# A gated attention and FFN block: a new order of the opening, weight loads moved, and unused multiplications on TensorE

## The chip, the cores and the metric

The kernel runs on one core of a Trainium2 chip. The metric is the device time of one execution in microseconds. The kernel is one program in which every engine has its own queue of instructions: TensorE (PE) multiplies, VectorE (DVE), ScalarE (ACT) and GpSimd (POOL) work on vectors, SyncE (SP) issues nearly all transfers. Engines wait for each other by semaphores only.

## The reference

Two sequences of 2048 tokens with 512 features (`x`), and for each a context of 128 rows. Cut to what matters:

```python
q = layernorm(x) @ Wq + bq ;  k = ctx @ Wk + bk ;  v = ctx @ Wv + bv     # 16 heads of 32
x = x + tanh(g_xattn) * (softmax(q k^T / sqrt(32)) v @ Wo + bo)
h = concat([layernorm(x), -layernorm(x)])
h = relu(s0 * h @ sign(k0)) * 2          # sign(k) is +1 where k is true, else -1; 1024 -> 2048
h = relu(s1 * h @ sign(k1)) * 2          # 2048 -> 2048
x = x + tanh(g_ffn) * s2 * h @ sign(k2)  # 2048 -> 512
```

## The kernel before

The tokens go through in 16 chunks of 256 (two tiles of 128 rows, TT = 2). Most values are kept as a high and a low float16 part, so that a product is two or three matmuls; the parts are made by ScalarE (high, by a copy) and VectorE (low, by a subtraction).

**The opening** handles the attention of chunk 0 and prepares what all chunks share. Its order is the list FIRST, written by hand: each engine walks the list and does its part of every item. The items are: LN and N1 (layernorm), T1 (turning the normed rows, by transposes on TensorE), CQ (splitting Wq: ScalarE Wq_hi L507, VectorE Wq_lo L938), CX (turning the context), Q n (queries of head group n, L1111 to L1113), QP n (their split, L537, L541, L793), K n (keys, L1059), KP n (their split: VectorE L915, ScalarE L499, GpSimd L426), KM n (keys masked by head: VectorE L931 for group 0, GpSimd L432 for the others), V (values of a batch, L1066), VP (their split, L921, L503, L923), SCALARS (gates and signs, VectorE L699 to L728), XB (bias of the residual, GpSimd L439), CO and CL (splitting Wo, L510 and L943), W0 (weights of the first FFN layer, L957 to L962), and for each of U = 8 units (four heads of 128 tokens) S (scores, L1094; VectorE takes the maximum, L797), EX (exponentials, ScalarE L520), PT (turning the probabilities: TensorE L1036, ScalarE L564, VectorE L744) and PV (the sum over values: TensorE L1120 and L1121, VectorE L752 to L759). CT, WO, N2 and T2 end the attention of the chunk. For unit k the loop over k puts S k+1, EX k and PV k-2, then what the table BETWEEN holds for k, then PT k-1.

**The loop** runs over FFN chunks f. SLOTS lists 44 steps of the FFN: eight L0 (first layer, L1210 and L1211), two L2P (end of the last chunk), then four groups q of seven L1 steps (second layer) with L2 steps (third layer, L1260 and L1261) of the group before between them. The attention of the next chunk is woven in by slot number (WEAVE, QUERIES): unit u has S at slot 10 + 2u, PS (split of the probabilities, L598 and L801, then a transposing transfer into PT) at 11 + 2u and PV at 15 + 2u. In chunk 0 the second layer is plain (`plain_product`, L1181 and L1183); from chunk 1 on it is done in seven products of block sums (L1243 and L1244), for which VectorE makes four sums of weight blocks for each group. `weight_step(q, step)` does that: step 0 makes signs of the loaded k1 (L973), steps 1 to 4 the sums (L977, L979, L983, L987). LATE_WEIGHTS says at which slot of chunk 0 or 1 each step stands. `load_k1(engine, q)` issues the two transfers of group q (L304).

W1 group 2 first holds Wv and group 3 holds Wq, so those loads come after their last use. In the SyncE queue the load of group 2 stands here, in chunk 0:

```python
                    if f == 0 and slot == ("L1", 1, P2):
                        sp.wait_ge(v_done, BATCHES)
                        load_k1(sp, 2)
```

That is slot 18; VectorE's step (2, 0), which waits for it, is also at slot 18.

## Time and profile before

| | |
|---|---|
| median of 3 runs | 1595.79 us (1595.55 to 1598.28) |
| the profiled execution: its time, its span | 1598.79 us, 1597.0 us |
| TensorE busy | 1533.0 us, 96% of the span |
| VectorE, ScalarE, GpSimd busy | 59%, 42%, 11% |
| mean granted clock of TensorE | 0.987 of full speed |

Times in the trace are microseconds from the start of the span. The granted clock is the share of TensorE's full 2.4 GHz that the chip let through; its lower level is 0.5, 1.2 GHz. The opening lasts until 88.26, when the first L1210 matmul starts; FFN chunk 0 lasts until 204.78.

### The profile page before, as it was taken

The numbers are of one execution on the slowest core, as the hardware profiler recorded it, in microseconds if no ns is written. First come the engines' busy times: TensorE is split into PE (matmuls) and PEld (weight loads), VectorE is DVE, ScalarE is ACT, GpSimd is POOL, SyncE is SP. The second block draws the span as 40 slices with busy tenths as digits, with TensorE's granted clock in tenths as the row PEclk, the third lists the DMA queues.
The fourth block names the chain that finished last, engine by engine and source line by source line (L and its number), as shares of the span: only waits on it lengthen the run. The fifth ranks groups of instructions, "written<-read, shape, count | busy, mean of one in ns | idle before, by whom it ended". The sixth has DMA issues, their size and how long they took to land.

```text
span 1597.0 us, 46107 instructions
## 1 busy us (share of the span) xinstructions
PE 1533.0 (96%) x19856; PEld 1302.6 (82%) x19856; DVE 939.8 (59%) x1938; ACT 674.1 (42%) x1568; POOL 168.0 (11%) x273
## 2 busy tenths in 40 slices
PE   5697989999999999999999999999999999999998
PEld 3476678888988888898888988888898888889887
DVE  4675875655656565565656556565655656565441
ACT  3343154452535445253544435254443525444231
POOL 2200202011020200102020110202011020201100
PEclk9799999999999999999999999999999999999999
DMA  7443225242332425343242423324252432424100
GB/s 224 96 103 73 47 71 90 48 94 61 94 67 63 99 46 99 58 94 68 79 83 51 97 55 97 65 81 81 51 98 55 97 65 75 87 50 98 28 29 14
DMA packets 278226, 120.95 MB, mean 76 GB/s; under 512 B 243464, under 2 KB 259848, under 8 KB 277896
## 3 DMA queue, kind: packets, MB, share of 16 engines
q1 hardware_dynamic: 275960, 117.48, 34.2%
q8 instruction: 156, 2.56, 0.7%
q10 hardware_dynamic: 2064, 0.53, 0.1%
q14 instruction: 46, 0.38, 0.1%
HBM read 37.76 MB, written 16.78 MB: 34 GB/s over the span
## 4 chain that ended last, share of the span: by engine, by line
PE 79%; DVE 9%; ACT 5%; issue 3%; DMA 3%; POOL 1%; SPq 0%; DVEq 0%; ACTq 0%; POOLq 0%
PE bank L1243 19%; PE bank L1244 19%; PE bank L1210 6%; PE bank L1211 6%; PE bank L1260 6%; PE bank L1261 6%; ACT Pf L520 2%; PE bank L1111 2%; PE bank L1112 2%; PE bank L1113 2%; PE bank L1127 2%; PE bank L1129 2%; PE bank L1128 2%; DVE nmax L797 2%; DMA PT<-Phl 1%
## 5 line engine op out<-in xcount | busy, mean ns | idle before, releaser
L1243 PE MATMUL bank<-H,W 128*128 128x128 f16 x6720 | 778.3, 219 | 5.2 <-ACT C L613 4.0
L1244 PE MATMUL bank<-H,W 128*128 128x128 f16 x6720 | 778.0, 219 | 0.0
L1243 PEld LDWEIGHTS bank<-H,W 128*128 128x128 fp8e5 x6720 | 655.4, 98 | 17.4 <-ACT C L613 9.8
L1244 PEld LDWEIGHTS bank<-H,W 128*128 128x128 fp8e5 x6720 | 657.4, 98 | 7.1
L1210 PE MATMUL bank<-hT,W 128*128 128x256 f16 x1024 | 228.5, 274 | 7.3 <-DVE h L852 5.4
L1211 PE MATMUL bank<-hT,W 128*128 128x256 f16 x1024 | 228.5, 274 | 0.0
L520 ACT ACTIVATE Pf<-bank,nmax 128x128 f32<-128x128 f32 x512 | 146.4, 369 | 155.2 <-DVE nmax L797 144.8
L1260 PE MATMUL bank<-W,h 128*128 128x512 fp8e5 x512 | 195.2, 381 | 1.6 <-DVE h L845 1.6
L1261 PE MATMUL bank<-W,h 128*128 128x512 fp8e5 x512 | 195.0, 381 | 0.0
L469 POOL TENSOR_TENSOR attn<-pvs 128x128 f32<-128x128 f32 x120 | 76.0, 633 | 1016.5 <-DVE pvs L810 1016.5
L837 DVE TENSOR_TENSOR C<-bank,C 128x256 f32<-128x256 f32 x180 | 76.3, 424 | 161.7 <-ACT C L613 89.8
L613 ACT ACTIVATE C<-bank 128x256 f32<-128x256 f32 x180 | 69.9, 388 | 212.8 <-PE bank L1244 212.8
L801 DVE SCALAR_TENSOR_TENSOR Phl<-Pf,Phl 128x512 f16<-128x512 f32 x120 | 82.6, 689 | 93.4 <-ACT Phl L598 93.3
L832 DVE TENSOR_TENSOR H<-Fp,H 128x896 f16<-128x896 f32 (+1 forms) x128 | 135.3, 1059 | 0.8 <-ACT H L604 0.8
L1210 PEld LDWEIGHTS bank<-hT,W 128*128 128x128 fp8e5 x1024 | 100.7, 98 | 19.6 <-issue 7.7
L638 ACT ACTIVATE Fp<-bank 128x512 f32<-128x512 f32 x128 | 76.5, 597 | 94.0 <-PE bank L1211 92.7
L609 ACT ACTIVATE H<-Fp 128x896 f16<-128x896 f32 x120 | 113.4, 945 | 1.8 <-DVE Fp L868 1.7
L845 DVE SCALAR_TENSOR_TENSOR h<-C,h 128x256 f16<-128x256 f32 x180 | 76.5, 425 | 60.8 <-ACT h L676 29.1
L1211 PEld LDWEIGHTS bank<-hT,W 128*128 128x128 fp8e5 x1024 | 100.6, 98 | 11.9
L797 DVE TENSOR_REDUCE nmax<-bank 128x4 f32<-128x512 f32 x128 | 87.6, 685 | 23.2 <-PE bank L1155 15.5
L1260 PEld LDWEIGHTS bank<-W,h 128*128 128x128 f16 x512 | 50.3, 98 | 53.6 <-issue 2.8
L1261 PEld LDWEIGHTS bank<-W,h 128*128 128x128 f16 x512 | 50.3, 98 | 51.8 <-issue 0.8
(129 smaller groups left out, 1919.4 us busy)
## 6 DMA issues: line engine op xcount, KB each, us to landing
Qst<-q_bounce SPq DMA_DIRECT2D x120, 128.0 KB, 2.8
Y<-in_x_dram SPq DMA_DIRECT2D x16, 512.0 KB, 3.8
...
```

Of the source, the lines that this page charges most:

```text
L520: last = nc.scalar.activation(Pf[:, n % 2, j * P:(j + 1) * P], bank[:, j * P:(j + 1) * P], ACT.Exp, bias=nmax[:, n % 2, j:j + 1], scale=1.0)
L609: nc.scalar.activation(H0[:, 0, i], Fp[:, i % 3, 1:8, :], ACT.Copy).then_inc(l0_hi, 1)
L638: nc.scalar.activation(Fp[:, n % 3, 0:4, :], banks[n % 3][:, :].rearrange("p (b n) -> p b n", b=4), ACT.Relu)\
L797: V_.tensor_reduce(nmax[:, n % 2, :], bank[:, :].rearrange("p (j k) -> p j k", j=4), AX.X, ALU.max, negate=True).then_inc(s_max, 1)
L801: V_.scalar_tensor_tensor(out=Phl[:, n % 2, 1, :], in0=Pf[:, n % 2, :], scalar=PS, in1=Phl[:, n % 2, 0, :], op0=ALU.mult, op1=ALU.subtract)\
L832: V_.tensor_tensor(H0[:, 1, i, rows, :], Fp[:, i % 3, of, :], H0[:, 0, i, rows, :], ALU.subtract)\
L1210: mm(o, w, hT[:, k, :], start=k == 0, stop=False)
L1211: last = mm(o, w, hT[:, KT + k, :], start=False, stop=k == KT - 1)
L1243: mm(o, w, H0[:, 0, i, b_of, :], start=first, stop=False, skip_group_check=True)
L1244: last = mm(o, w, H0[:, 1, i, b_of, :], start=False, stop=i == PAIRS - 1, skip_group_check=True)
L1260: mm(banks[3 + t][:, :], hi, w2, start=q == 0 and h == 0 and jj == 0, stop=False)
L1261: last = mm(banks[3 + t][:, :], lo, w2, start=False, stop=q == GROUPS - 1 and h == 1 and jj == 1)
```

## The change

It rewrites the order of the opening, moves two loads and several weight steps, and adds multiplications whose result nobody reads.

- The table BETWEEN becomes EARLY (ahead of S and EX of the unit) and MIDDLE. KP and KM stand early, K one or more units ahead of its KP. QD is a new name for VectorE's part of QP, so that it can stand later. SCALARS stands ahead of Q 0; the product of bo with its gate is an item of its own, BO.
- V of a batch is two halves of 256 columns, V 0 and V 1 for batch 0.
- EX n of the opening waits for PT n-2 on TensorE, no longer for its low part on VectorE.
- SyncE issues the k1 load of group 3 right behind group 0's, and that of group 2 at slot 9 instead of 18.
- Three weight steps, (2, 4), (3, 2) and (3, 3), go from chunk 0 to chunk 1; others stand at every second slot.
- WARM n is n matmuls of 512 columns on zeros in PT, into bank 5: 14 ahead of T1, 6 ahead of Q 0, 5 ahead of WO 0, 7 behind T2.

```diff
+    FIRST = first(("LN", 0), ("LN", 1), ("N1", 0), ("N1", 1), ("WARM", 14), ("T1", 0), ("T1", 1), ("CQ", 0), ("CQ", 1), ("CQ", 2),
+                  ("CQ", 3), ("CX", 0), ("CX", 1), ("WARM", 6), ("SCALARS", 0), ("Q", 0), ("Q", 1), ("QP", 0), ("QD", 0),
...
+    EARLY = {1: first(("KP", 2), ("KM", 2)), 2: first(("QP", 2), ("VP", 0)), 3: first(("KP", 3), ("KM", 3)),
...
+    MIDDLE = {0: first(("V", 0), ("K", 2)), 1: first(("V", 1), ("Q", 2)), 2: first(("QD", 2), ("K", 3)),
...
     for k in range(U + 2):
-        FIRST += first(*((kind, k + ahead) for kind, ahead in (("S", 1), ("EX", 0), ("PV", -2)) if 0 <= k + ahead < U))
-        FIRST += BETWEEN.get(k, [])
+        FIRST += EARLY.get(k, [])
+        FIRST += first(*((kind, k + ahead) for kind, ahead in (("S", 1), ("EX", 0)) if 0 <= k + ahead < U))
+        FIRST += first(("PV", k - 2)) if k > 2 else []
+        FIRST += MIDDLE.get(k, [])
         FIRST += first(("PT", k - 1)) if 0 <= k - 1 < U else []
+        FIRST += first(("PV", 0)) if k == 2 else []
         FIRST += first(("CT", k - 8)) if k >= 8 else []
...
-                     26: (1, 2), 28: (3, 0), 29: (1, 3), 31: (1, 4), 32: (2, 1), 34: (2, 2), 35: (2, 3), 36: (2, 4),
-                     37: (3, 1), 39: (3, 2), 41: (3, 3)}, {9: (3, 4)})
+                     26: (1, 2), 28: (3, 0), 30: (1, 3), 32: (1, 4), 34: (2, 1), 36: (2, 2), 38: (2, 3), 40: (3, 1)},
+                    {11: (2, 4), 15: (3, 2), 19: (3, 3), 23: (3, 4)})
...
+            sp.wait_ge(wq_lo, KT)
+            load_k1(sp, 3)
             sp.wait_ge(n1_ready, NT)
...
             load_k1(sp, 1)
-            sp.wait_ge(wq_lo, KT)
-            load_k1(sp, 3)
...
-                    if f == 0 and slot == ("L1", 1, P2):
-                        sp.wait_ge(v_done, BATCHES)
+                    if f == 0 and slot == ("L2P", GROUPS - 1, 1):
+                        sp.wait_ge(v_done, 2 * BATCHES)
                         load_k1(sp, 2)
...
-                if a or n >= 2:
+                if a == 0 and n >= 2:
+                    act.wait_ge(p_turned, n - 1)
+                if a:
                     act.wait_ge(p_lo, nth(a, NU, n - 2))
...
+            V_.memset(PT[:, 1], 0.0).then_inc(zeros_made, 1)
...
+                if kind == "WARM":
+                    pe.wait_ge(zeros_made, 1)
+                    idle = PT[:, 1].rearrange("p a n -> p (a n)")
+                    for _ in range(n):
+                        mm(banks[5][:, :], idle[:, 0:P], idle[:, 0:4 * P], start=True, stop=True)
```

TensorE's queue at its start, from T1 over CX (the rows that read R) to the first query matmul, before:

```order
L1036 MATMUL bank<-ident,xn 128x128 [waits n1_ready]
L1036 MATMUL bank<-ident,xn 128x128 x3
L1036 MATMUL bank<-ident,xn 128x128 [waits n1_ready]
L1036 MATMUL bank<-ident,xn 128x128 x3
L1036 MATMUL bank<-ident,R 128x128 [waits ctx_in,ident_made]
L1036 MATMUL bank<-ident,R 128x128 x7
L1111 MATMUL bank<-xT,Wq_hi 128x256 [waits first_lo,wq_lo,ctx_taken]
```

The same place in the changed kernel (its lines are numbered some 9 to 16 higher; L1055 is WARM):

```order
L1055 MATMUL bank<-PT 128x512 [waits zeros_made]
L1055 MATMUL bank<-PT 128x512 x13
L1045 MATMUL bank<-ident,xn 128x128 [waits n1_ready]
L1045 MATMUL bank<-ident,xn 128x128 x3
L1045 MATMUL bank<-ident,xn 128x128 [waits n1_ready]
L1045 MATMUL bank<-ident,xn 128x128 x3
L1045 MATMUL bank<-ident,R 128x128 [waits ctx_in,ident_made]
L1045 MATMUL bank<-ident,R 128x128 x7
L1055 MATMUL bank<-PT 128x512 [waits zeros_made]
L1055 MATMUL bank<-PT 128x512 x5
```

The multiplications of zeros stand ahead of T1 and behind CX; nothing else moved between them. VectorE's queue between the low parts of PT 0 and PT 1 (L744), before; the rows from L699 to L728 are SCALARS with the product of bo:

```order
L699 TENSOR_SCALAR c<-scal 128x2 [waits scalars_in]
L701 TENSOR_SCALAR c<-c 128x2 [waits const_step]
L704 TENSOR_SCALAR c<-c 128x1 [waits const_tanh,const_step]
L705 TENSOR_SCALAR c<-c 128x1
L706 TENSOR_SCALAR c<-c,scal 128x1
L707 TENSOR_TENSOR c<-scal,c 128x2
L709 TENSOR_SCALAR c<-c 128x1 [waits const_step]
L712 TENSOR_SCALAR bo_b<-bo_b,c 128x512 [waits bo_in]
L719 TENSOR_SCALAR w_mask<-scal 128x1
L723 SCALAR_TENSOR_TENSOR w_mask<-w_mask 128x1 [waits const_step] x2
L728 TENSOR_TENSOR w_mask<-w_mask,eleventh_mask 128x1 [waits masks_made,const_step]
L744 SCALAR_TENSOR_TENSOR PT<-bank,PT 128x512 [waits p_hi,const_step]
```

And between the same two rows (L749) in the changed kernel:

```order
L749 SCALAR_TENSOR_TENSOR PT<-bank,PT 128x512 [waits p_hi]
L926 TENSOR_TENSOR Phl<-bank,Phl 128x512 [waits v_done,bv_in]
L928 SCALAR_TENSOR_TENSOR V<-Phl,V 128x16x32 [waits v_hi]
L802 TENSOR_REDUCE nmax<-bank 128x4 [waits s_done]
L798 TENSOR_TENSOR Qhl<-Qf,Qhl 128x256 [waits q_split]
L749 SCALAR_TENSOR_TENSOR PT<-bank,PT 128x512 [waits p_hi]
```

SCALARS has left this place; the split of V (L926, L928) and the low part of Q 2 (L798) stand in it. SyncE's queue in FFN chunk 0 around the k1 load of group 2 (L304), before:

```order
L367 DMA Qst<-q_bounce 64x1024 [waits s_done,q_kept1]
L367 DMA Qst<-q_bounce 64x1024
L373 DMA_TRANSPOSE PT<-Phl 128x8x128 [waits p_lo,pv_done]
L304 DMA W<-in_L_ffn_k_dram 128x16x64 [waits v_done]
L304 DMA W<-in_L_ffn_k_dram 128x16x64
L373 DMA_TRANSPOSE PT<-Phl 128x8x128 [waits p_lo,pv_done] x4
```

And after (the load is L309, q_bounce and Qst are the queries on their way, PT the probabilities):

```order
L372 DMA Qst<-q_bounce 64x1024 [waits s_done,q_kept1]
L372 DMA Qst<-q_bounce 64x1024
L309 DMA W<-in_L_ffn_k_dram 128x16x64 [waits v_done]
L309 DMA W<-in_L_ffn_k_dram 128x16x64
L363 DMA q_bounce<-Qhl 4x32x256 [waits q_lo]
L363 DMA q_bounce<-Qhl 4x32x256
L378 DMA_TRANSPOSE PT<-Phl 128x8x128 [waits p_lo,pv_done]
```

The load went from behind the fourth PT transfer to ahead of the first, and ahead of the last query's transfer.

## Rows read from the trace of the kernel before

**Rows 1.** The page of the profile: span and busy time of the engines.

```profile
span 1597.0 us, 46107 instructions
...
PE 1533.0 (96%) x19856; PEld 1302.6 (82%) x19856; DVE 939.8 (59%) x1938; ACT 674.1 (42%) x1568; POOL 168.0 (11%) x273
```

**Rows 2.** Busy time by stretch, in us from the start of the span.

```profile
core 0: us, PE busy (x) PEld busy (x) DVE busy (x) ACT busy (x) POOL busy (x), PEclk, DMA share, GB/s
42.30:72.90 30.60, 19.99 (x142) 15.48 (x140) 16.52 (x39) 13.72 (x37) 5.08 (x7) 0.74 0.51 121
132.30:204.80 72.50, 56.36 (x441) 41.12 (x439) 54.67 (x61) 14.09 (x32) 10.86 (x14) 0.91 0.31 63
204.80:297.40 92.60, 92.17 (x1219) 78.39 (x1220) 56.12 (x116) 41.01 (x96) 9.80 (x16) 0.98 0.36 72
```

**Rows 3.** A wait of TensorE before 88.3 us: total, times, longest.

```profile
PE bank L1094 <- POOL h L432: 9.9, 2, 5.0
```

**Rows 4.** Busy time and granted clock of TensorE alone, by stretch.

```profile
core 0: us, PE busy (x), PEclk, DMA share, GB/s
8.55:12.20 3.65, 3.65 (x16) 1.00 0.87 267
15.00:20.00 5.00, 5.00 (x24) 1.00 1.00 384
30.80:32.10 1.30, 1.30 (x13) 1.00 0.45 75
142.40:147.10 4.70, 4.70 (x22) 0.51 0.30 56
204.80:208.60 3.80, 3.80 (x19) 0.52 0.00 0
```

**Rows 5.** Timeline of VectorE, opening: start, length, instruction, idle before, releaser.

```profile
18.61 0.42 DVE L793 TENSOR_TENSOR Qhl<-Qf,Qhl 128x256 f16<-128x256 f32 x1 [3.13 <-ACT Qf L541]
...
34.26 0.69 DVE L744 SCALAR_TENSOR_TENSOR PT<-bank,PT 128x512 f16<-128x512 f32 x1 [0.59 <-ACT PT L564]
...
37.56 0.16 DVE L699 TENSOR_SCALAR c<-scal 128x2 f32<-128x2 f32 x1
...
42.32 0.69 DVE L744 SCALAR_TENSOR_TENSOR PT<-bank,PT 128x512 f16<-128x512 f32 x1
...
63.31 0.69 DVE L744 SCALAR_TENSOR_TENSOR PT<-bank,PT 128x512 f16<-128x512 f32 x1 [0.78 <-ACT PT L564]
...
67.34 0.69 DVE L744 SCALAR_TENSOR_TENSOR PT<-bank,PT 128x512 f16<-128x512 f32 x1 [0.92 <-ACT PT L564]
...
72.16 0.69 DVE L744 SCALAR_TENSOR_TENSOR PT<-bank,PT 128x512 f16<-128x512 f32 x1 [1.52 <-ACT PT L564]
```

**Rows 6.** Timeline of ScalarE, one step of the opening.

```profile
64.10 1.14 ACT L520 ACTIVATE Pf<-bank,nmax 128x128 f32<-128x128 f32 x4 [0.82 <-DVE PT L744]
...
66.07 0.61 ACT L510 ACTIVATE Wo_hi<-H 128x512 f16<-128x512 f32 x1
...
66.71 0.60 ACT L564 ACTIVATE PT<-bank 128x512 f16<-128x512 f32 x1
```

**Rows 7.** Timeline of TensorE: three waits in the first FFN chunk.

```profile
142.40 0.24 PE L1120 MATMUL bank<-V,PT 128*128 128x65 f16 x1 [7.54 <-ACT Pf L520]
...
164.43 0.22 PE L1120 MATMUL bank<-V,PT 128*128 128x65 f16 x1 [2.76 <-DMA PT<-Phl]
...
204.78 0.37 PE L1210 MATMUL bank<-hT,W 128*128 128x256 f16 x1 [5.38 <-DVE h L852]
```

**Rows 8.** Timeline of the SyncE queue: two loads of k1.

```profile
15.77 12.10 SPq L304 DMA_DIRECT2D W<-in_L_ffn_k_dram  x2
...
132.34 2.23 SPq L304 DMA_DIRECT2D W<-in_L_ffn_k_dram  x2
```

**Rows 9.** Timeline of VectorE, first FFN chunk: two weight steps.

```profile
139.28 1.29 DVE L973 TENSOR_SCALAR W<-W,w_mask 128x2048 uint32<-128x2048 uint32 x1 [8.34 <-DMA W<-in_L_ffn_k_dram]
...
201.75 2.28 DVE L983 TENSOR_TENSOR W<-W 128x2048 fp8e5<-128x2048 fp8e5 x1
```

More of the change, by code:

```diff
@@ new lines, in gated_block_kernel @@
+    EARLY = {1: first(("KP", 2), ("KM", 2)), 2: first(("QP", 2), ("VP", 0)), 3: first(("KP", 3), ("KM", 3)),
+             4: first(("QP", 3)), 5: first(("KP", 4)), 6: first(("KP", 5)), 7: first(("KP", 6)), 8: first(("KP", 7))}
+    MIDDLE = {0: first(("V", 0), ("K", 2)), 1: first(("V", 1), ("Q", 2)), 2: first(("QD", 2), ("K", 3)),
+              3: first(("Q", 3), ("BO", 0)), 4: first(("QD", 3), ("XB", 0), ("K", 4), ("CO", 0)),
+              5: first(("XB", 1), ("K", 5), ("CL", 0), ("CO", 1)), 6: first(("K", 6), ("CL", 1), ("CO", 2)),
+              7: first(("K", 7), ("CL", 2), ("CO", 3)), 8: first(("CL", 3)), 9: first(("W0", 0))}
@@ L131, in gated_block_kernel @@
         FIRST += first(("CT", k - 8)) if k >= 8 else []
     FIRST += [(1, ("LN", 0)), (1, ("LN", 1))]
-    FIRST += first(("WO", 0), ("WO", 1), ("N2", 0), ("N2", 1), ("V", 1), ("T2", 0), ("T2", 1))
+    FIRST += first(("WARM", 5), ("WO", 0), ("WO", 1), ("N2", 0), ("N2", 1), ("V", 2), ("V", 3), ("T2", 0), ("T2", 1),
+                   ("WARM", 7))
     FIRST_ITEMS = [item for a, item in FIRST if a == 0]
@@ L729, in follow_sign @@
                     .then_inc(const_step, 1)
-                dve.wait_ge(const_step, 9)
+                dve.wait_ge(const_step, 8)
             def attend_first(item):
@@ L790, in attend @@
                             in1=xs[:, k % 2, 0, :], op0=ALU.mult, op1=ALU.subtract).then_inc(xs_lo, 1)
-                if kind == ("QP" if first else "Q"):
+                if kind == ("QD" if first else "Q"):
                     dve.wait_ge(q_split, nth(a, NG, n))
@@ L1045, in begin @@
                 before = user_before(FIRST_ITEMS, FIRST_BANK, item)
-                if before is not None:
+                if before is not None and not (kind == "V" and n % 2):
                     pe.wait_ge(*released(before, 0))
@@ L1064, in begin @@
                         pe.wait_ge(wv_in, 16)
+                    b, half = divmod(n, 2)
+                    columns = slice(half * D // 2, (half + 1) * D // 2)
                     for k in range(KT):
-                        last = mm(bank[:, :], ctxT[:, k, n * P:(n + 1) * P], Wv_f[:, k, :],
-                                  start=k == 0, stop=k == KT - 1)
+                        last = mm(bank[:, columns], ctxT[:, k, b * P:(b + 1) * P], Wv_f[:, k, columns],
+                                  start=k == 0, stop=k == KT - 1, skip_group_check=True)
                     last.then_inc(v_done, 1)
```

31 lines of the change are left out of this document (12 added, 19 removed).

## The prediction

> **What bounds the kernel now.** I read the page first: TensorE is busy for 1533.0 of the 1597.0 us of the span [rows 1]. The busy times by stretch say where the other time is. From 204.8 us on a chunk takes about 92.6 us, and TensorE is busy for 92.17 of them: nothing that frees another engine can help there. The opening is different: from 42.3 to 72.9 us TensorE is busy for 19.99 of 30.60 us, at a mean granted clock of 0.74. The second part of FFN chunk 0, from 132.3 to 204.8 us, has 56.36 busy of 72.50 us, and VectorE is busy for 54.67 of them [rows 2]. Since everything behind is bound by TensorE, a microsecond taken out of either stretch ends the kernel a microsecond earlier, if no new wait takes its place.
>
> The waits of TensorE and the timelines name the causes. In the opening it waited 9.9 us, in two pieces, for the masked keys of GpSimd [rows 3]. The step from one low part of PT to the next is the beat of the softmax units: PT 0 stands at 34.26, PT 1 at 42.32, PT 7 at 72.16 us [rows 5], so seven steps took 37.9 us. In the first of them VectorE did SCALARS, from 37.56 to the PT row at 42.32, 4.8 us. In chunk 0 there are three waits: 7.54, 2.76 and 5.38 us [rows 7]. The first has its root in VectorE, which sat 8.34 us for a k1 load [rows 9] that SyncE issued only at 132.34 [rows 8]. After two of them the clock is at its lower level for busy stretches of 4.7 and 3.8 us [rows 4].
>
> **The change part by part.** The sums are made against the profiled execution, 1598.79 us, which is 1.8 above its span and 3.0 above the median of the three runs.
>
> *Up to the first scores.* Fourteen zero matmuls fill the start. At the lower clock 24 matmuls of 256 columns took 5.00 us, at the higher 12 took 1.30 us [rows 4], so one of 512 columns is 0.42 or 0.22 us. Fourteen are at most 5.9 us and end before the first transposes, which wait for VectorE's xn until 8.5 us: they cost nothing. If the clock is up when Q 0 and Q 1 come, these 24 matmuls take 2.6 instead of 5.0 us: 2.4 off. CX 0 no longer stands between the four splits of Wq: 0.6 off. SCALARS, 3.7 us without the product of bo, now stands ahead of the split of Q 0, where VectorE sat 3.13 us [rows 5]; its small instructions ran while GpSimd masked keys, so I take half a microsecond of it as uncovered. The six zero matmuls in front of Q 0 are 1.3 to 2.5 us long and have VectorE's Wq splits as cover (TensorE waited 2.8 us there); were that gone they would cost that much. I take 2.5 off, bounds 0 and 4.
>
> *The eight softmax units.* With SCALARS out and keys split one unit ahead, a step should shrink to what VectorE and ScalarE do in series. From the rows: low part of PT 0.6 us, VectorE's part of KP and the hop 0.4, ScalarE's KP 0.2, EX 1.0 (from 64.10 on, without its pipelined end), the Wo split 0.6, the high part of PT 0.6 [rows 5, 6]: 3.4 us. The steady steps of before, such as 63.31 to 67.34, took 4.0, since PV on VectorE stood in the chain in front of KP. Seven steps at 3.5 are 24.5 us. TensorE then works less than half of the last two steps, as it did before, so I expect the lower clock there, with a key block and a PT turn at half speed on the chain: 1.5 us more. 26.0 instead of 37.9 us: 11.9 off, bounds 8 and 14. GpSimd's masks of 2.1 us start right after the keys and end two units before their scores; they are what is late next if the keys are.
>
> *From PT 7 to the first layer.* The path stays. Five zero matmuls stand ahead of WO 0, whose operands are ready: 1.1 to 2.1 us in the way, of which part comes back since WO 0 then runs sooner at full clock. The seven behind T2 are 1.5 to 2.9 us and lie beside the splits of T2, for which TensorE waited 1.9 us; without that cover they cost it all. V as halves has the same columns. I take 0.4 lost, bounds 3 lost and 1.5 won. The opening gives 2.5 + 11.9 - 0.4 = 14.0 us.
>
> *The load of group 2.* It goes to slot 9, nine steps of some 2 us before its use, against 6.3 us that it took to land. The 7.54 us wait goes, and with it 4.7 us at the lower clock, half of which is 2.35: 9.9 off. In SyncE's queue two query pieces and the PT transfers now stand behind it. It held the queue for 2.23 us at its old place and, in a full queue, a like pair for 12.10 [rows 8]. I take 1 us lost, bounds 0 and 8.
>
> *The late wait of 2.76 us* and a short one of 0.46 before it come from VectorE catching up after its 8.34 us; they have 3.2 us at the lower clock behind them, 1.6 lost. Of these 4.8 I take 3.5 as gone.
>
> *Three weight steps less in chunk 0.* Each is 2.28 us [rows 9], and VectorE's last h row before chunk 1 stood behind them. The end wait of 5.38 us falls to the bare split of the last block, which I put at 1.5 us, the length of ScalarE's high part and VectorE's low part: 3.9 off, and 3.8 us at the lower clock become 1.9: 5.8 off. In chunk 1 VectorE has 56.12 busy of 92.6 us [rows 2]; three steps make it 63. They stand on the slots of PS, so each can delay a PT transfer by 2.28 us, with four slots to its PV. I take 1.5 lost, bounds 0 and 6.8 (all three in full).
>
> Chunk 0 and 1 give 9.9 - 1 + 3.5 + 5.8 - 1.5 = 16.7 us. The whole is 14.0 + 16.7 = 30.7 off 1598.79, which is 1568.1; at the median, 1595.8 - 30.7 = 1565.
>
> *A rule against the warming.* From 8.55 to 12.2 us TensorE turned blocks without a gap, and at 15 to 20 us it still ran 24 matmuls in 5.00 us, the pace of the lower clock, though the profile has no reading of the granted clock that early and prints 1.00 [rows 4]. The Trainium skill, "TensorE: Matmul & The Clock Gate", Part 4: PE-mode transpose, says that transposes don't count as TensorE activity in the way of matmuls. By that rule, the trace agrees, the gain of the fourteen would be lost again during T1 and CX.
>
> **The rivals.**
> - *The warming doesn't hold.* The clock falls between the fourteen and Q 0, since transposes and a 2 us gap lie between. For it: 3.7 us of transposes did not raise the clock. Against it: six zero matmuls follow at once. Then the 2.4 us of Q stay, and the five ahead of WO 0 cost their 2 us: 1565 + 2.4 + 2 = 1569. The rule of the Trainium skill quoted above says this.
> - *Chunk 0 stays bound by VectorE.* It is busy for 54.67 of 72.50 us there [rows 2]; less 6.8 it has 47.9, but its steps alternate with waits for ScalarE. If the steps between slots 18 and 28 still make TensorE wait, the 3.5 don't come and chunk 1 costs its 6.8: 1565 + 3.5 + 5.3 = 1574.
> - *Keys on the chain of the units.* If each KP waits for its K on TensorE, a step gets the PV, the key block and a hop, 1.3 us at full clock: seven steps make 9 us, 1574. Against it: K stands a whole step ahead.
> - *Slower.* The early load holds SyncE's queue with queries and PT transfers behind it. At 12.10 us, less some 3.5 of slack, TensorE waits 8.6, which only takes the place of the wait removed: 1574. It ends above before only if the queue stands for more than 35 us, the 30.7 won and the slack; no row shows a pair of loads of 1 MB held so long.
> - *No effect:* the opening's gain is given back by a k1 or x transfer that is as late as before. The loads are issued by semaphores that move with the opening, and TensorE waited for no load of the opening.
>
> **How the numbers follow.** The forecast as summed has a chance of 0.6, the first rival 0.12, the second 0.12, the third 0.08, the slower one 0.03 (of which 0.02 above before), no effect 0.02, a mixture beyond these 0.03. The bounds of the terms that are free (opening 4 either way, chunk 0 and 1 some 5) give 1556 to 1574 for the forecast; up to 1578 takes in most of the rivals. A measurement of this kernel can tell a change of 0.2%, 3.2 us. Faster by more: 0.96; within: 0.02; slower: 0.02.
>
> **What would show it.** L1226, the first layer, starts near 74 us instead of 88.3. SCALARS lies before 20 us, the PT rows follow each other by 3.4 to 4 us. Query matmuls before 20 us run at 0.11 us each, or at 0.21 if the first rival is right. The wait of 7.54 us is gone and VectorE's step (2, 0) has no transfer ahead of it. The second chunk starts near 174 us. From there chunks of 92 to 93 us, the first of them with small waits where the three steps lie. The prediction is wrong if the first layer starts after 79 us, or if waits of several microseconds for PT transfers stand in chunk 0 or 1.

## The result, and the profile after

The changed kernel takes 1571.78 us, the median of four runs (1570.59 to 1572.85), against 1597.00 us of the kernel before beside it (1595.55 to 1598.28): a ratio of 0.9842, interval 0.9825 to 0.9859, 1.6% faster. The profiled execution took 1571.66 us.

The page of the changed kernel, the lines that answer to [rows 1]:

```profile
span 1569.8 us, 46204 instructions
...
PE 1530.4 (97%) x19904; PEld 1302.2 (83%) x19904; DVE 938.9 (60%) x1939; ACT 672.3 (43%) x1568; POOL 168.8 (11%) x273
```

The span is 27.2 us shorter and TensorE's busy time 2.6 us, but the small second number hides a larger one. The kernel without the zero matmuls (the first experiment below) is as fast, and its page has TensorE busy for 1522.1 us, 10.9 less than before, at a mean granted clock of 0.996 instead of 0.987. So some 11 us of the gain are busy time, most of it presumably matmuls that no longer run at the lower clock, and some 16 are idle time that is gone; the zero matmuls fill 8.3 us of what is left idle without them.

The busy times by stretch of the changed kernel, for the stretches that answer to those of [rows 2]: PT 0 to PT 7, the second part of chunk 0, and chunk 1 to the point that lies 92.7 us behind its start.

```profile
core 0: us, PE busy (x) PEld busy (x) DVE busy (x) ACT busy (x) POOL busy (x), PEclk, DMA share, GB/s
30.60:55.70 25.10, 16.38 (x157) 12.26 (x156) 21.66 (x47) 15.60 (x45) 6.72 (x9) 1.00 0.57 135
118.00:177.70 59.70, 53.75 (x435) 39.71 (x433) 46.92 (x55) 13.94 (x32) 12.83 (x14) 0.97 0.26 52
177.70:270.40 92.70, 88.38 (x1188) 75.75 (x1189) 60.99 (x117) 40.15 (x95) 10.44 (x16) 1.00 0.33 73
```

The reader sees three things. PT 0 to PT 7, seven steps, takes 25.10 us at a granted clock of 1.00; the row of before starts at PT 1, and its six steps had 30.60 us at 0.74. The end of chunk 0 is 59.70 us with 5.95 idle, where 72.50 had 16.14 idle. And chunk 1, which had 0.43 us idle in 92.60, now has 4.32 in 92.70: something was pushed there.

The timeline of TensorE in the changed kernel: the first matmul of the first layer in chunks 0, 1 and 2 (L1226), and the two longest waits (in brackets, with what ended them). They answer to [rows 7].

```profile
73.92 0.27 PE L1226 MATMUL bank<-hT,W 128*128 128x256 f16 x1 [0.37 <-DVE hT L743]
...
140.94 0.19 PE L1136 MATMUL bank<-V,PT 128*128 128x65 f16 x1 [2.68 <-DMA PT<-Phl]
...
177.69 0.27 PE L1226 MATMUL bank<-hT,W 128*128 128x256 f16 x1 [1.63 <-DVE h L857]
...
221.58 0.23 PE L1259 MATMUL bank<-H,W 128*128 128x128 f16 x1 [2.34 <-ACT C L620]
...
274.84 0.27 PE L1226 MATMUL bank<-hT,W 128*128 128x256 f16 x1
```

The waits of TensorE before 73.95 us, to be held against [rows 3]: those for GpSimd's masked keys are not among them any more. What is left between the units is TensorE waiting for VectorE's low part of each PT, the beat of the softmax units itself.

```profile
PE bank L1136 <- DVE PT L749: 6.8, 6, 1.6
PE bank L1045 <- DVE attn L764: 1.9, 2, 1.2
```

VectorE's opening, to be held against [rows 5]: SCALARS starts at 15.70 instead of 37.56, PT 0 stands at 30.61, PT 1 at 34.13, PT 7 at 55.71.

```profile
15.70 0.17 DVE L706 TENSOR_SCALAR c<-scal 128x2 f32<-128x2 f32 x1 [0.35 <-DMA scal<-in_L_ffn_s_dram]
...
30.61 0.69 DVE L749 SCALAR_TENSOR_TENSOR PT<-bank,PT 128x512 f16<-128x512 f32 x1 [3.41 <-ACT PT L571]
...
34.13 0.68 DVE L749 SCALAR_TENSOR_TENSOR PT<-bank,PT 128x512 f16<-128x512 f32 x1
...
55.71 0.68 DVE L749 SCALAR_TENSOR_TENSOR PT<-bank,PT 128x512 f16<-128x512 f32 x1
```

Seven steps took 25.1 us instead of 37.9. SyncE's queue, against the second row of [rows 8]: the k1 load of group 2 is issued at 96.12 instead of 132.34 and holds the queue for 2.43 us.

```profile
96.12 2.43 SPq L309 DMA_DIRECT2D W<-in_L_ffn_k_dram  x2
```

Before the experiments, the account by place, from the starts of the first layer in each chunk (before: 88.26, 204.78, 299.50 us; after: the rows above):

| | before | after | difference |
|---|---|---|---|
| opening | 88.26 | 73.92 | -14.34 |
| chunk 0 | 116.52 | 103.77 | -12.75 |
| chunk 1 | 94.72 | 97.15 | +2.43 |
| chunk 2 to the end | 1297.5 | 1295.0 | -2.5 |

The last row has the same code in both kernels. In the profiles of the twelve experiments it lies between 1294.0 and 1296.3 us, so some 2 us of the 27.2 belong to the one execution of before that was profiled. The other three rows give 24.7 us, and the medians 25.2.

### The profile page after: what moved, and what is told of

It is laid out like the page before. It is cut to its first block, busy times and chain, and to the rows that moved or that the text cites. A ratio compares the mean times of both kernels' runs of the same rounds, so it can differ in the third digit from the quotient of the medians.

```text
span 1569.8 us, 46204 instructions
## 1 busy us (share of the span) xinstructions
PE 1530.4 (97%) x19904; PEld 1302.2 (83%) x19904; DVE 938.9 (60%) x1939; ACT 672.3 (43%) x1568; POOL 168.8 (11%) x273
## 4 chain that ended last, share of the span: by engine, by line
PE 87%; DVE 6%; ACT 3%; DMA 2%; issue 1%; SPq 0%; POOL 0%; DVEq 0%; ACTq 0%; POOLq 0%
PE bank L1259 22%; PE bank L1260 22%; PE bank L1226 7%; PE bank L1227 7%; PE bank L1276 7%; PE bank L1277 6%; PE bank L1143 2%; PE bank L1144 2%; PE bank L1145 2%; PE bank L1127 2%; PE bank L1129 2%; PE bank L1128 2%; PE bank L1171 1%; PE bank L1199 1%; PE bank L1197 1%
## 5 line engine op out<-in xcount | busy, mean ns | idle before, releaser
L1226 PE MATMUL bank<-hT,W 128*128 128x256 f16 x1024 | 226.8, 273 | 2.0 <-DVE h L857 1.6
L527 ACT ACTIVATE Pf<-bank,nmax 128x128 f32<-128x128 f32 x512 | 145.9, 368 | 139.2 <-DVE nmax L802 137.5
L806 DVE SCALAR_TENSOR_TENSOR Phl<-Pf,Phl 128x512 f16<-128x512 f32 x120 | 82.5, 688 | 92.0 <-ACT Phl L605 91.9
L1226 PEld LDWEIGHTS bank<-hT,W 128*128 128x128 fp8e5 x1024 | 100.2, 98 | 14.2 <-issue 2.7
L1227 PEld LDWEIGHTS bank<-hT,W 128*128 128x128 fp8e5 x1024 | 100.2, 98 | 11.3
L802 DVE TENSOR_REDUCE nmax<-bank 128x4 f32<-128x512 f32 x128 | 87.5, 683 | 17.5 <-PE bank L1171 16.6
```

The source lines that it names most:

```text
L527: last = nc.scalar.activation(Pf[:, n % 2, j * P:(j + 1) * P], bank[:, j * P:(j + 1) * P], ACT.Exp, bias=nmax[:, n % 2, j:j + 1], scale=1.0)
L802: V_.tensor_reduce(nmax[:, n % 2, :], bank[:, :].rearrange("p (j k) -> p j k", j=4), AX.X, ALU.max, negate=True).then_inc(s_max, 1)
L806: V_.scalar_tensor_tensor(out=Phl[:, n % 2, 1, :], in0=Pf[:, n % 2, :], scalar=PS, in1=Phl[:, n % 2, 0, :], op0=ALU.mult, op1=ALU.subtract)\
L1226: mm(o, w, hT[:, k, :], start=k == 0, stop=False)
L1227: last = mm(o, w, hT[:, KT + k, :], start=False, stop=k == KT - 1)
```

## The experiments

The positions are those of each kernel's profiled execution. Each group was timed beside the kernel before on one chip; the ratio is to that, and kernels of different groups are best compared by it.

| kernel | median us | ratio, interval | first layer at | chunk 1 at | chunk 0 |
|---|---|---|---|---|---|
| changed kernel | 1571.78 | 0.9842, 0.9825 to 0.9859 | 73.92 | 177.69 | 103.77 |
| no zero matmuls | 1572.11 | 0.9844, 0.9831 to 0.9858 | 73.56 | 177.27 | 103.71 |
| only the 14 | 1570.66 | 0.9834, 0.9821 to 0.9848 | 73.12 | 176.93 | 103.81 |
| only the 6 | 1570.67 | 0.9833, 0.9820 to 0.9847 | 74.08 | 177.62 | 103.54 |
| without the 5 and 7 | 1570.58 | 0.9834, 0.9820 to 0.9847 | 75.33 | 179.05 | 103.72 |
| load back at slot 18 | 1580.01 | 0.9895, 0.9880 to 0.9910 | 74.42 | 186.31 | 111.89 |
| old weight slots | 1573.68 | 0.9851, 0.9836 to 0.9865 | 75.77 | 183.21 | 107.44 |
| before, load at slot 9 | 1588.85 | 0.9951, 0.9934 to 0.9968 | 88.74 | 196.52 | 107.78 |
| before, SCALARS early | 1596.10 | 0.9998, 0.9988 to 1.0007 | 87.76 | 204.22 | 116.46 |
| SCALARS back behind PT 0 | 1573.02 | 0.9843, 0.9829 to 0.9858 | 73.17 | 176.96 | 103.79 |
| keys late | 1580.69 | 0.9893, 0.9876 to 0.9909 | 80.84 | 184.41 | 103.57 |
| five steps on odd slots | 1568.26 | 0.9816, 0.9801 to 0.9830 | 74.06 | 174.33 | 100.27 |
| combined | 1566.44 | 0.9803, 0.9788 to 0.9817 | 72.78 | 173.04 | 100.26 |

### Do the zero matmuls give anything?

Four kernels leave out all of them, or keep only some. All:

```diff
-    FIRST = first(("LN", 0), ("LN", 1), ("N1", 0), ("N1", 1), ("WARM", 14), ("T1", 0), ("T1", 1), ("CQ", 0), ("CQ", 1), ("CQ", 2),
-                  ("CQ", 3), ("CX", 0), ("CX", 1), ("WARM", 6), ("SCALARS", 0), ("Q", 0), ("Q", 1), ("QP", 0), ("QD", 0),
+    FIRST = first(("LN", 0), ("LN", 1), ("N1", 0), ("N1", 1), ("T1", 0), ("T1", 1), ("CQ", 0), ("CQ", 1), ("CQ", 2),
+                  ("CQ", 3), ("CX", 0), ("CX", 1), ("SCALARS", 0), ("Q", 0), ("Q", 1), ("QP", 0), ("QD", 0),
...
-    FIRST += first(("WARM", 5), ("WO", 0), ("WO", 1), ("N2", 0), ("N2", 1), ("V", 2), ("V", 3), ("T2", 0), ("T2", 1),
-                   ("WARM", 7))
+    FIRST += first(("WO", 0), ("WO", 1), ("N2", 0), ("N2", 1), ("V", 2), ("V", 3), ("T2", 0), ("T2", 1))
```

> The changed kernel without any of the 32 zero multiplications. Theory (the new order and the moved loads are the gain, the warming is worth little): Q 0 and Q 1 run at 0.21 us a matmul, the first layer starts 0 to 2.5 us later than the 73.9 us of the changed kernel, the kernel takes 1572 to 1574 us. Rival (the warming carries a good part of the 14 us of the opening): first layer after 77 us, 1576 us or more.

The second keeps only the 14 ahead of T1:

```diff
-                  ("CQ", 3), ("CX", 0), ("CX", 1), ("WARM", 6), ("SCALARS", 0), ("Q", 0), ("Q", 1), ("QP", 0), ("QD", 0),
+                  ("CQ", 3), ("CX", 0), ("CX", 1), ("SCALARS", 0), ("Q", 0), ("Q", 1), ("QP", 0), ("QD", 0),
...
-    FIRST += first(("WARM", 5), ("WO", 0), ("WO", 1), ("N2", 0), ("N2", 1), ("V", 2), ("V", 3), ("T2", 0), ("T2", 1),
-                   ("WARM", 7))
+    FIRST += first(("WO", 0), ("WO", 1), ("N2", 0), ("N2", 1), ("V", 2), ("V", 3), ("T2", 0), ("T2", 1))
```

> Only the fourteen ahead of T1 are kept. In the changed kernel the clock rose at 5.7, fell at 9.1 and rose again at 12.6 us. Theory (the fourteen are lost again before Q 0, only the six behind CX matter): query matmuls start at 0.21 us, first layer as in the kernel without any. Rival (transposes hold the clock, the fourteen alone do): query matmuls at 0.11 us from the first on, first layer some 2 us earlier than in the kernel without any.

The third keeps only the 6 ahead of Q 0:

```diff
-    FIRST = first(("LN", 0), ("LN", 1), ("N1", 0), ("N1", 1), ("WARM", 14), ("T1", 0), ("T1", 1), ("CQ", 0), ("CQ", 1), ("CQ", 2),
+    FIRST = first(("LN", 0), ("LN", 1), ("N1", 0), ("N1", 1), ("T1", 0), ("T1", 1), ("CQ", 0), ("CQ", 1), ("CQ", 2),
...
-    FIRST += first(("WARM", 5), ("WO", 0), ("WO", 1), ("N2", 0), ("N2", 1), ("V", 2), ("V", 3), ("T2", 0), ("T2", 1),
-                   ("WARM", 7))
+    FIRST += first(("WO", 0), ("WO", 1), ("N2", 0), ("N2", 1), ("V", 2), ("V", 3), ("T2", 0), ("T2", 1))
```

> Only the six behind CX are kept. Theory (the six together with the transposes ahead of them raise the clock before Q 0): most of the 24 query matmuls at 0.11 us, first layer at 73 to 74 us. Rival (without the fourteen the six are too few): queries at 0.21 us until some 17 us, first layer 1 to 2.5 us later.

The fourth keeps both of these and leaves out the 5 ahead of WO 0 and the 7 behind T2:

```diff
-    FIRST += first(("WARM", 5), ("WO", 0), ("WO", 1), ("N2", 0), ("N2", 1), ("V", 2), ("V", 3), ("T2", 0), ("T2", 1),
-                   ("WARM", 7))
+    FIRST += first(("WO", 0), ("WO", 1), ("N2", 0), ("N2", 1), ("V", 2), ("V", 3), ("T2", 0), ("T2", 1))
```

> The fourteen and the six are kept, the five ahead of WO 0 and the seven behind T2 are out. Theory: the five only delayed WO 0, whose operands were ready (59.2 to 61.3 us), at the lower clock, and the clock rises at the same time without them; WO 0 starts 2 us earlier, of which half is paid back at the lower clock, the seven cost nothing: first layer 1 us earlier, near 72.9 us, kernel 1 us faster. Rival (the five bring the clock up earlier): first layer not earlier or up to 2 us later.

The four medians lie between 1570.58 and 1572.11 us, the changed kernel's at 1571.78, and all intervals overlap: the zero matmuls are worth nothing that can be measured. Of what was expected, the first kernel's time (1572 to 1574) came, and its first layer is not later but 0.4 us earlier. In the second the clock, up at 4.9 us, held through the transposes and fell only at 15.2, so the fourteen were not lost before Q 0, and yet most query matmuls ran at the lower clock. In the third it rose at 13.3 and held for all 24, as the theory had it. TensorE alone in four stretches of the changed kernel, with its granted clock, shows how each piece went:

```profile
core 0: us, PE busy (x), PEclk, DMA share, GB/s
8.60:11.90 3.30, 3.30 (x17) 0.53 0.94 279
15.00:17.40 2.40, 2.40 (x24) 1.00 0.99 383
59.30:61.30 2.00, 2.00 (x6) 0.50 0.28 82
142.40:145.60 3.20, 3.20 (x17) 0.54 0.17 34
```

The 24 matmuls of Q 0 and Q 1 took 2.40 us (15.00 to 17.40) against the 5.00 of [rows 4]: the gain that was meant is there. By the transposes from 8.6 us on the clock was down again (0.53; it fell at 9.1, behind a wait of 2.0 us), and it was back at 12.6. The five ahead of WO 0 ran from 59.22 to 61.35 us at 0.50: the clock had fallen at 56.9, and they only stood in the way. The last row is what the wait of 2.68 us left behind it: 3.20 us of matmuls at the lower clock. In the kernel without any, key group 1 starts at 21.82 instead of 20.08 us and CT 1 ends the units at 60.09 instead of 58.34, 1.75 later; but WO 0 then follows at once (60.97), where in the changed kernel it starts at 61.35. In these two profiles the first two pieces win 1.7 us and the third gives it back: the first layer starts at 73.92 with them and at 73.56 without. The fourth kernel does not bear out the win: it keeps the 14 and the 6, but its clock fell at 21.4 us, CT 1 stands at 61.08, and its first layer starts at 75.33 where 72.9 was expected. What the five cost is seen in the last kernel of this document, which leaves them out and whose clock went as in the changed kernel (down at 56.6 instead of 56.9, up at 63.4 instead of 63.8). Its WO 0 and that of the changed kernel:

```profile
59.20 0.63 PE L1142 MATMUL bank<-Wo_hi,xT 128*128 128x512 f16 x1
...
61.35 0.63 PE L1143 MATMUL bank<-Wo_hi,xT 128*128 128x512 f16 x1
```

PT 7 stands at 55.69 and 55.71, CT 1 at 58.33 and 58.34, the first layer at 72.78 and 73.92. The five took 2.15 us and cost 1.1, the 1 us of the fourth kernel's theory: without them WO 0 starts sooner, but more of it runs at the lower clock.

The same kernel holds a surprise at its start. Its TensorE timeline, without zero matmuls: eight transposes of xn, and the first query matmuls.

```profile
8.49 1.97 PE L1044 MATMUL bank<-ident,xn 128*128 128x128 f32 x8 [8.49 <-DVE xn L783]
...
14.88 0.28 PE L1126 MATMUL bank<-xT,Wq_hi 128*128 128x256 f16 x1 [2.80 <-DVE hT L912]
15.00 0.27 PE L1127 MATMUL bank<-xT,Wq_hi 128*128 128x256 f16 x1
```

Nothing but transposes (those of the context follow until 12.1 us) ran before 14.88 us, yet the first two query matmuls start 0.12 us apart, the pace of the higher clock; its trace has the clock going up at 12.0 and down at 15.4. The stretch right behind, with the granted clock at its lower level of 1.2 GHz:

```profile
core 0: us, PE busy (x), PEclk, DMA share, GB/s
15.50:18.70 3.20, 3.20 (x17) 0.50 1.00 387
```

So here the rise came with transposes alone ahead of it, and the clock fell again behind the wait of 2.80 us.

### The load of group 2

In the changed kernel the load goes back to slot 18:

```diff
-                    if f == 0 and slot == ("L2P", GROUPS - 1, 1):
+                    if f == 0 and slot == ("L1", 1, P2):
```

> The changed kernel with the k1 load of group 2 back at slot 18. Theory (the early load is worth the wait of 7.5 us and the lower clock behind it): VectorE's step (2, 0) waits some 8 us for the transfer again, TensorE some 7, the kernel takes 8 to 10 us more, 1580 to 1582 us. Rival (VectorE's alternation with ScalarE would have made TensorE wait there anyway): 3 to 6 us more, 1575 to 1578 us.

Chunk 0 is 8.1 us longer and the median 8.2, as the theory had it. TensorE's timeline of this kernel has the old wait back:

```profile
127.69 0.24 PE L1136 MATMUL bank<-V,PT 128*128 128x65 f16 x1 [7.42 <-ACT Pf L527]
```

The other direction, the load alone brought forward in the kernel before:

```diff
-                    if f == 0 and slot == ("L1", 1, P2):
+                    if f == 0 and slot == ("L2P", GROUPS - 1, 1):
```

> The kernel before with the load of group 2 at slot 9 and nothing else changed. Theory: the 7.5 us wait and half of 4.7 us at the lower clock go, other waits of the chunk stay: 8 to 10 us faster than before, 1587 to 1589 us. Rival (VectorE, late by itself, takes the gain back at the end of the chunk, where it already makes TensorE wait 5.4 us): 3 to 6 us faster.

The median falls by 8.0 us and chunk 0 by 8.7. The wait of 7.54 us is gone. The other two waits of [rows 7] are not:

```profile
156.11 0.19 PE L1120 MATMUL bank<-V,PT 128*128 128x65 f16 x1 [2.73 <-DMA PT<-Phl]
...
196.52 0.37 PE L1210 MATMUL bank<-hT,W 128*128 128x256 f16 x1 [5.36 <-DVE h L852]
```

2.73 and 5.36 us, as before 2.76 and 5.38. VectorE no longer sits 8.34 us for a transfer in this kernel, so that cannot be the cause of the 2.76.

### The weight steps

The changed kernel with the slots of before for the weight steps:

```diff
-                     26: (1, 2), 28: (3, 0), 30: (1, 3), 32: (1, 4), 34: (2, 1), 36: (2, 2), 38: (2, 3), 40: (3, 1)},
-                    {11: (2, 4), 15: (3, 2), 19: (3, 3), 23: (3, 4)})
+                     26: (1, 2), 28: (3, 0), 29: (1, 3), 31: (1, 4), 32: (2, 1), 34: (2, 2), 35: (2, 3), 36: (2, 4),
+                     37: (3, 1), 39: (3, 2), 41: (3, 3)}, {9: (3, 4)})
```

> The changed kernel with the weight steps where they were (three more in chunk 0, one instead of four in chunk 1). Theory (in the first chunk the three cost a wait of some 4 us at its end and a lowered clock, in the second their absence saves 3 us of small waits): 1 to 4 us slower than the changed kernel. Rival (they only changed places): within 1 us.

The wait at the end of chunk 0 is back, with the lower clock from 180.5 to 187.3 us around it:

```profile
183.21 0.37 PE L1226 MATMUL bank<-hT,W 128*128 128x256 f16 x1 [5.37 <-DVE h L857]
```

Chunk 0 is 3.7 us longer than in the changed kernel, and chunk 1 2.4 shorter (94.76 instead of 97.15) though it carries the lower clock's loss. What the move of three steps wins in chunk 0 it mostly pays back in chunk 1: the medians are 1.9 us apart, and their intervals overlap.

### SCALARS and the keys

In the kernel before, SCALARS alone moves ahead of Q 0:

```diff
-                  ("CQ", 2), ("CQ", 3), ("CX", 1), ("Q", 0), ("Q", 1), ("QP", 0), ("K", 0), ("KP", 0), ("K", 1),
+                  ("CQ", 2), ("CQ", 3), ("CX", 1), ("SCALARS", 0), ("Q", 0), ("Q", 1), ("QP", 0), ("K", 0), ("KP", 0), ("K", 1),
...
-               2: first(("QP", 2), ("KP", 2), ("KM", 2), ("SCALARS", 0)), 3: first(("Q", 3), ("K", 3), ("XB", 0)),
+               2: first(("QP", 2), ("KP", 2), ("KM", 2)), 3: first(("Q", 3), ("K", 3), ("XB", 0)),
```

> The kernel before with SCALARS (the product of bo with it) ahead of Q 0 and nothing else changed. Theory (its 4.8 us on VectorE were on the chain of the softmax units): first layer 4 to 5 us earlier, near 84 us. Rival (the masked keys of GpSimd are late by as much and take its place): 0 to 2 us earlier, and the wait of 5 us for them stays.

A ratio of 0.9998: nothing, as the rival had it; the first layer starts at 87.76 instead of 88.26. PT 1 now follows PT 0 after 4.24 us instead of 8.06, but PT 2 follows PT 1 after 8.64 instead of 5.19: what the first step wins, the second gives back to the wait for the masked keys. That stands as in [rows 3], now twice 4.8 us:

```profile
PE bank L1094 <- POOL h L432: 9.7, 2, 4.8
```

In the changed kernel SCALARS moves back behind PT 0:

```diff
-                  ("CQ", 3), ("CX", 0), ("CX", 1), ("WARM", 6), ("SCALARS", 0), ("Q", 0), ("Q", 1), ("QP", 0), ("QD", 0),
+                  ("CQ", 3), ("CX", 0), ("CX", 1), ("WARM", 6), ("Q", 0), ("Q", 1), ("QP", 0), ("QD", 0),
...
-    MIDDLE = {0: first(("V", 0), ("K", 2)), 1: first(("V", 1), ("Q", 2)), 2: first(("QD", 2), ("K", 3)),
+    MIDDLE = {0: first(("V", 0), ("K", 2)), 1: first(("V", 1), ("Q", 2)), 2: first(("QD", 2), ("K", 3), ("SCALARS", 0)),
```

> The changed kernel with SCALARS back in unit 2, behind K 3. In the kernel before, moving it alone gained 0.5 us, since the wait of 4.8 us for GpSimd's masked keys stayed. Theory (the two delays lay beside each other, and with the keys early the one for SCALARS comes to light): the step in which it stands grows by 2.5 to 4 us, first layer at 76 to 78 us, 1574 to 1576 us. Rival (it is covered in unit 2 as well): first layer within 0.7 us of 73.9.

VectorE's timeline of this kernel, where SCALARS starts, its two instructions of L728, and PT 1 behind them:

```profile
33.60 0.16 DVE L706 TENSOR_SCALAR c<-scal 128x2 f32<-128x2 f32 x1
...
34.81 0.35 DVE L728 SCALAR_TENSOR_TENSOR w_mask<-w_mask 128x1 uint32<-128x1 uint32 x2
...
35.39 0.69 DVE L749 SCALAR_TENSOR_TENSOR PT<-bank,PT 128x512 f16<-128x512 f32 x1
```

SCALARS takes 1.8 us there, and PT 0 to PT 1 is 5.3 us instead of 3.5. CT 1 comes 1.75 us later (60.09), but the first layer does not (73.17 against 73.92); the clock in this execution was up from 42.0 us to the end of the opening. The median is 1.2 us higher, below the 1574 of the theory, and the intervals overlap. The theory had SCALARS too long: of the 4.8 us in the kernel before, 1.1 were the product of bo, and 1.7 more went into two small instructions beside GpSimd (last section).

The third kernel keeps all else and puts keys 2 and 3, with their splits and masks, where the kernel before had them:

```diff
-    EARLY = {1: first(("KP", 2), ("KM", 2)), 2: first(("QP", 2), ("VP", 0)), 3: first(("KP", 3), ("KM", 3)),
+    EARLY = {2: first(("QP", 2), ("VP", 0)),
...
-    MIDDLE = {0: first(("V", 0), ("K", 2)), 1: first(("V", 1), ("Q", 2)), 2: first(("QD", 2), ("K", 3)),
-              3: first(("Q", 3), ("BO", 0)), 4: first(("QD", 3), ("XB", 0), ("K", 4), ("CO", 0)),
+    MIDDLE = {0: first(("V", 0)), 1: first(("V", 1), ("Q", 2), ("K", 2)), 2: first(("QD", 2), ("KP", 2), ("KM", 2)),
+              3: first(("Q", 3), ("K", 3), ("BO", 0)), 4: first(("QD", 3), ("KP", 3), ("KM", 3), ("XB", 0), ("K", 4), ("CO", 0)),
```

> The changed kernel with K, KP and KM of groups 2 and 3 where they stood before (K one unit later, their splits and masks behind the scores). Theory (the early keys are most of the opening's gain): TensorE waits again for GpSimd's masks ahead of S 4 and S 6, 3 to 5 us each, first layer at 80 to 83 us, 1578 to 1581 us. Rival (with SCALARS gone the masks are in time even so): waits under 1.5 us each, first layer before 77 us.

The waits for GpSimd's masks return:

```profile
PE bank L1110 <- POOL h L437: 7.2, 2, 3.9
```

7.2 us in two pieces; the first layer starts 6.9 us later and the median is 8.9 higher. Both numbers and both waits are as the theory had them. Keys ahead of their unit are the largest piece of the opening's 14.3 us that was taken away by itself.

### The step on the wrong side of the maximum

Of the waits of chunk 0 the changed kernel keeps 0.53, 0.35, 0.75 and 2.68 us between 124 and 141. Here VectorE and ScalarE take turns, and the weight steps of slots 16 to 26 stand between the split of one unit and the maximum of the next. Five of them move one slot on:

```diff
-    LATE_WEIGHTS = ({6: (0, 0), 11: (1, 0), 13: (0, 1), 16: (0, 2), 18: (2, 0), 20: (0, 3), 22: (1, 1), 24: (0, 4),
-                     26: (1, 2), 28: (3, 0), 30: (1, 3), 32: (1, 4), 34: (2, 1), 36: (2, 2), 38: (2, 3), 40: (3, 1)},
+    LATE_WEIGHTS = ({6: (0, 0), 11: (1, 0), 13: (0, 1), 17: (0, 2), 18: (2, 0), 21: (0, 3), 23: (1, 1), 25: (0, 4),
+                     27: (1, 2), 28: (3, 0), 30: (1, 3), 32: (1, 4), 34: (2, 1), 36: (2, 2), 38: (2, 3), 40: (3, 1)},
```

> The changed kernel with five weight steps of chunk 0 one slot later (16, 20, 22, 24, 26 to 17, 21, 23, 25, 27), so that each runs on VectorE behind the maximum of the scores, while ScalarE takes the exponentials. Theory (in chunk 0 VectorE alternates with ScalarE in a beat of 5.36 us for two slots, of which 1.3 us is VectorE waiting for ScalarE; a step put into that wait shortens the beat to some 4 us): the waits of 0.53, 0.35, 0.75 and 2.68 us and the lowered clock behind the last go, chunk 0 takes 99 to 101 instead of 103.8 us, 1567 to 1569 us. Rival (VectorE's sum of work bounds the stretch, whatever the order): chunk 0 within 1 us of 103.8.

Chunk 0 takes 100.27 instead of 103.77 us. One unit of the changed kernel, on the timelines of VectorE and, last row, of ScalarE:

```profile
119.60 0.69 DVE L806 SCALAR_TENSOR_TENSOR Phl<-Pf,Phl 128x512 f16<-128x512 f32 x1 [1.32 <-ACT Phl L605]
...
120.21 2.28 DVE L991 TENSOR_TENSOR W<-W 128x2048 fp8e5<-128x2048 fp8e5 x1
...
122.41 0.68 DVE L802 TENSOR_REDUCE nmax<-bank 128x4 f32<-128x512 f32 x1
...
124.96 0.69 DVE L806 SCALAR_TENSOR_TENSOR Phl<-Pf,Phl 128x512 f16<-128x512 f32 x1 [0.72 <-ACT Phl L605]
...
123.12 1.14 ACT L527 ACTIVATE Pf<-bank,nmax 128x128 f32<-128x128 f32 x4 [3.07 <-DVE nmax L802]
```

And of the kernel with the steps one slot on:

```profile
118.58 0.69 DVE L806 SCALAR_TENSOR_TENSOR Phl<-Pf,Phl 128x512 f16<-128x512 f32 x1 [1.32 <-ACT Phl L605]
...
119.19 0.68 DVE L802 TENSOR_REDUCE nmax<-bank 128x4 f32<-128x512 f32 x1
...
120.39 2.28 DVE L991 TENSOR_TENSOR W<-W 128x2048 fp8e5<-128x2048 fp8e5 x1
...
123.14 0.68 DVE L806 SCALAR_TENSOR_TENSOR Phl<-Pf,Phl 128x512 f16<-128x512 f32 x1
...
119.91 1.14 ACT L527 ACTIVATE Pf<-bank,nmax 128x128 f32<-128x128 f32 x4 [0.87 <-DVE nmax L802]
```

In the first the step (2.28 us) stands ahead of the maximum (L802), and ScalarE's exponentials (L527) sat 3.07 us for it; the low part of the probabilities (L806) comes every 5.36 us. In the second the maximum goes first, ScalarE waits 0.87, the exponentials run beside the step, and the low parts are 4.56 us apart (4 were expected). No instruction is gone: two rows have changed places. The waits of 0.53, 0.35 and 0.75 are gone, that of 2.68 is 1.39, a new one of 1.39 for xT stands behind it, and the clock does not fall. Of the 3.5 us, 1.5 are idle time of TensorE in the chunk (6.57 to 5.05) and 2.0 are busy time (97.20 to 95.22), at a granted clock of 1.00 instead of 0.98. Its four runs, 1567.72 to 1569.64 us, all lie below those of the changed kernel, though the intervals of the ratios just touch.

The last kernel adds other slots in chunk 1 and leaves out the 5 and 7 zero matmuls:

```diff
-    FIRST += first(("WARM", 5), ("WO", 0), ("WO", 1), ("N2", 0), ("N2", 1), ("V", 2), ("V", 3), ("T2", 0), ("T2", 1),
-                   ("WARM", 7))
+    FIRST += first(("WO", 0), ("WO", 1), ("N2", 0), ("N2", 1), ("V", 2), ("V", 3), ("T2", 0), ("T2", 1))
...
-                    {11: (2, 4), 15: (3, 2), 19: (3, 3), 23: (3, 4)})
+                    {9: (2, 4), 13: (3, 2), 22: (3, 3), 31: (3, 4)})
```

> The same five steps, the four steps of chunk 1 at slots 9, 13, 22 and 31 instead of 11, 15, 19 and 23 (where VectorE has no sum or rest of the second layer to take), and no zero multiplications ahead of WO 0 and behind T2. Theory: the waits of 0.62, 2.34, 0.60 and 0.68 us in chunk 1 go as well, another 3 us, and 0 to 1 us in the opening: 1563 to 1566 us. Rival (the steps only make other rows of chunk 1 late): no faster than the kernel with the five steps alone.

TensorE's timeline of this kernel, the starts of chunks 1 and 2 and the longest wait between them:

```profile
173.04 0.27 PE L1225 MATMUL bank<-hT,W 128*128 128x256 f16 x1 [1.63 <-DVE h L856]
...
229.76 0.22 PE L1258 MATMUL bank<-H,W 128*128 128x128 f16 x1 [1.25 <-DVE h L849]
...
268.81 0.27 PE L1225 MATMUL bank<-hT,W 128*128 128x256 f16 x1
```

Chunk 1 is 95.77 us instead of 97.15, and its wait of 2.34 us for ScalarE's C is gone; 1.25 and 0.82 are left, so the theory had too much in saying that all four go. 1566.44 us, 0.4 above the expected range, ratio 0.9803 (0.9788 to 0.9817), is the fastest of all, clear of the changed kernel's interval, and 1.8 us below the kernel with the odd slots, which is not told apart from it.

## Why the prediction was right, and where it was not

It named 1565 us and a range of 1556 to 1578; 1571.78 is in the range and 6.8 above the forecast, nearer to the 1574 of the second rival, whose mechanism holds in chunk 0. Against its own profiled execution it had 30.7 us off, and 27.2 came, of which some 2 lie behind chunk 1 in code that did not change.

- **Opening, 14.0 forecast, 14.34 measured.** The parts are less exact than their sum, and that the sum is this close is luck. Up to PT 0 it is 3.65 us (34.26 to 30.61) instead of 2.5, the seven steps won 12.8 instead of 11.9, and PT 7 to the first layer is 18.2 us where it was 16.1: 2.1 lost, not 0.4. The five zero matmuls ahead of WO 0 are 1.1 of that. The other 1.0 goes with a lower clock of 6.8 us (56.9 to 63.8), which the term did not have: it lasts 3.4 us there before (75.5 to 78.9) and in the kernel without zero matmuls, and both need 16.1 us from PT 7 to the first layer. Besides, three experiments have the changed kernel's opening unchanged (load back at slot 18, old weight slots, odd slots), and their first layer starts at 74.42, 75.77 and 74.06 us: one profile gives the opening to some 2 us only.
- **Seven steps, 26.0 us forecast, 25.1 measured.** The steps are 3.52, 5.10, 3.30, 3.71, 3.34, 3.37 and 2.76 us. The 1.5 us for a lower clock in the last two did not come (1.00 from PT 0 to PT 7). In their place the second step is 1.6 us longer than the 3.5 of the sum: VectorE worked through it without a gap, it holds PV of two units, and two of its instructions, beside GpSimd's masks, took 1.5 us more than elsewhere (last section). SCALARS, priced at 3.7 us, took 1.8 ahead of Q 0.
- **The chain behind the 11.9** holds: late keys bring 7.2 us of waits back, SCALARS moved alone brings nothing, and SCALARS put back costs its 1.8 us at its place. The third rival (keys on the chain) is wrong, since between PT 0 and PT 7 neither VectorE nor ScalarE waits for a K. How the other half of the opening's gain, 7.4 us, divides over the halves of V, the PV moved, QD and the wait of EX was not measured.
- **The zero matmuls** did for Q what was forecast (2.40 instead of 5.00 us), and the kernel is no faster for them. The first rival said that the clock falls between the fourteen and Q 0. It did fall, at 9.1 us, but it was up again at 12.6, beside the six, so Q ran fast and the rival's price did not come. The sentence that rests on the Trainium skill, "TensorE: Matmul & The Clock Gate", Part 4: PE-mode transpose, ended in the trace agreeing. That reading fell: in the kernel without zero matmuls, and in the kernel before with the early load (clock up at 11.3), transposes alone were ahead of the rise. Where page and measurement differ, the measurement decides.
- **The load, 9.9 less 1 for the queue, 8.9 forecast.** 8.1 us taken from one side and 8.7 from the other. In the queue it cost 2.43 us of issue and no wait for PT that can be laid to it: the one of 2.68 us is 2.69 with the load back at slot 18. What is missing to the 9.9 stands in part in two waits for exponentials of 0.5 and 0.4 us, which both kernels with the early load have (0.53 and 0.35, 0.54 and 0.35) and both with the late one lack. The slower rival did not come.
- **The end wait, 5.8 forecast with its clock.** 5.38 became 1.63 (3.75 off, 3.9 forecast), and no lower clock follows it in chunk 1, where before it was busy for 3.8 us at half speed, 1.9 lost.
- **"Of these 4.8 I take 3.5 as gone": the step that failed.** The wait of 2.76 us was laid to VectorE catching up after its 8.34 us. With the load early it stayed, at 2.73 us in the kernel before and at 2.68 in the changed one; the clock, which fell behind it from 142.3 to 145.7 us in the changed kernel, stayed up in the other. The stretch is held up by the beat of VectorE and ScalarE, the mechanism of the second rival: the odd slots take 3.5 us off chunk 0, as much as the term claimed. From the low part at 107.93 us to that at 136.74 the changed kernel takes 28.8 us, and the same stretch with the odd slots (108.12 to 133.50) 25.4. This explains the wait itself only by half, since 1.39 us of it are left there and a wait of 1.39 for xT follows; what holds these was not tested. With the term that failed, the forecast of 16.3 us for chunk 0 (9.9 - 1 + 3.5 + 3.9) came out as 12.75.
- **Chunk 1, 1.5 forecast.** It is 2.43 us longer though 1.9 of clock came back: 4.3 us. The mechanism, small waits where the three steps lie, was right (0.62, 2.34, 0.60 and 0.68 us), and the old slots show the price from the other side: chunk 1 without the three steps has no wait over 0.3 us. The term was sized near its lower bound where the middle of 0 to 6.8 would have been closer.

The sum of the misses, 3.6 in chunk 0 and 2.8 in chunk 1 less 0.3 in the opening, is 6.1 us; 30.7 less these is 24.6, and the three rows of the account give 24.7.
